# Routed expert layer: every expert on every token, or tiles of 256 rows of one expert each

## The reference

```python
x = x + ga * attention(h)                       # B, S, E = 4, 2048, 256
h = layernorm(x) * (1 + cb) + sb                # cb, sb, gb: one row of 256 per batch entry
probs = softmax(h @ gate_w.T + gate_b)          # over 8 experts
_, topi = top_k(probs, 2)
cw = einsum('bske,bsk->bse', one_hot(topi, 8), probs[..., :2])
out = 0
for e in range(8):
    t = relu(h @ w1[e] + b1[e]); t = relu(t @ w2[e] + b2[e]); t = t @ w3[e] + b3[e]
    out = out + cw[..., e:e+1] * t
x = x + gb * out
```

## Time and profile before

| | us |
|---|---|
| runs of the kernel before, median (lowest to highest) | 4469.58 (4466.67 to 4480.1) |
| the profiled execution, its own time | 4463.85 |
| its span, first to last instruction | 4462.3 |
| TensorE busy in the span | 3969.2 (89%) |
| VectorE, ScalarE, GpSimd busy | 2795.3, 1907.5, 1132.6 |
| granted clock of TensorE, mean | 0.965 |

### The profile page before, as it was taken

How to read it: one execution, slowest core, us unless ns; L and a number is a source line. 1 busy time by engine, 2 the same in 40 slices (tenths; PEclk the granted TensorE clock), 3 DMA queues, 4 the chain that set the end, 5 groups by cost and what they waited for, 6 DMA issues and landing times. The chain is left out here.

```text
span 4462.3 us, 182622 instructions
## 1 busy us (share of the span) xinstructions
PE 3969.2 (89%) x79696; PEld 3129.7 (70%) x79696; DVE 2795.3 (63%) x4823; ACT 1907.5 (43%) x2398; POOL 1132.6 (25%) x922
## 2 busy tenths in 40 slices
PE   6947999999999999999999999986699999999998
PEld 4537887778888778888778888775366566566565
DVE  5845666644667753566763666660678677687774
ACT  1301334453333454233444234444455555556555
POOL 1024222122221113221112322100133343333333
PEclk8968999998999999999999999998799999999999
DMA  4761110003110003110003100002411112112100
GB/s 131 207 158 48 31 30 25 17 27 96 33 32 22 22 21 103 34 33 22 21 22 96 40 23 28 17 6 48 98 25 43 30 25 48 25 30 43 24 10 10
DMA packets 212117, 201.07 MB, mean 45 GB/s; under 512 B 92048, under 2 KB 156156, under 8 KB 211324
## 3 DMA queue, kind: packets, MB, share of 16 engines
q1 hardware_dynamic: 195068, 154.30, 13.3%
q0 software_dynamic: 16256, 35.02, 2.6%
HBM read 128.69 MB, written 59.29 MB: 42 GB/s over the span
## 5 line engine op out<-in xcount | busy, mean ns | idle before, releaser
L739 ACT ACTIVATE att_pt<-att_ps 128x1024 f32<-128x1024 f32 x560 | 573.9, 1025 | 1246.0 <-PE att_ps L763 1245.9
L706 DVE TENSOR_TENSOR att_acc<-att_pm,att_acc 128x512 f32<-128x512 f32 x864 | 570.2, 687 | 361.9 <-PE att_pm L760 356.9
L714 DVE TENSOR_TENSOR att_acc<-att_pm,att_acc 128x512 f32<-128x512 f32 x1056 | 665.9, 684 | 171.2 <-PE att_pm L770 164.7
L760 PE MATMUL att_ps<-att_qx,table_x 68*128 68x64 f16 x8960 | 721.1, 194 | 0.0
L763 PE MATMUL att_ps<-att_qz,table_z 128*128 128x64 f16 x8960 | 718.3, 193 | 0.0
L742 ACT ACTIVATE att_pt<-att_ps 128x1024 f32<-128x1024 f32 x528 | 515.1, 1023 | 372.3 <-PE att_ps L770 371.5
L763 PEld LDWEIGHTS att_ps<-att_qz,table_z 128*128 128x128 f16 x8960 | 614.5, 99 | 0.0
L760 PEld LDWEIGHTS att_ps<-att_qx,table_x 68*128 68x128 f16 x8960 | 611.8, 98 | 0.1
L826 PE MATMUL att_po<-att_pt,att_vn 128*32 128x128 f32 x17408 | 593.6, 277 | 0.2 <-ACT att_pt L739 0.2
L664 POOL DMA_DIRECT2D s_m<-att_mrow x64 | 34.3, 535 | 1850.9 <-DVE att_mrow L722 1823.5
L756 PE MATMUL att_ps<-att_qs,att_kn 113*128 113x64 f16 x8960 | 451.6, 193 | 42.8 <-DMA att_qs<-s_m 32.6
(11 more groups left out here) (173 smaller groups left out, 5377.3 us busy)
## 6 DMA issues: line engine op xcount, KB each, us to landing
att_qe<-s_q SPq DMA_DIRECT2D x256, 128.0 KB
s_v<-prj_vx SPq DMA_DIRECT2D x32, 512.0 KB, 3.8
att_vn<-s_v SPq DMA_DIRECT2D x64, 256.0 KB, 3.4
s_o<-att_on POOLq DMA_DIRECT2D x64, 256.0 KB, 3.5
ffn_heads<-s_o SPq DMA_DIRECT2D x64, 256.0 KB, 5.0
att_qs<-s_q SPq DMA_DIRECT2D x128, 66.0 KB
prj_x<-in_x POOLq DMA_DIRECT2D x16, 512.0 KB, 4.6
att_kn<-s_k SPq DMA_DIRECT2D x128, 64.0 KB, 2.4
```

The costliest lines, as they stand in the source:

```text
L706: dve.tensor_tensor(held, got, held, ALU.max).then_inc(mx_done, 1)
L714: dve.tensor_tensor(held, got, held, ALU.max).then_inc(mx_done, 1)
L739: act.activation(pt[:, k % 2, :, t * 64:t * 64 + 64].rearrange("p h (x c) -> p x h c", x=2), ps[t][:, :, :].rearrange("p x (h c) -> p x h ...
L760: last = pe.matmul(groups[:, :, g], keep["table_x"][:, y:y + P], qx[0:G * D + G, s, x * (XQ // G) + g], start=False, stop=(g == XQ // G - ...
```

## The change

The last phase is replaced by `phase_moe`, written out without a loop, in three stages.

First, 16 chunks of 512 tokens are prepared as before (the sums are now inverted once for all chunks, with a pass through DRAM) and routed: `count` finds with matmuls against a triangle and a matrix of ones how many earlier tokens chose the same expert, which gives each token a row in the region of each of its two experts (`s_h` in DRAM). GpSimd scatters the normalised rows there, eight indirect transfers of 128 rows of 1 KB a chunk. `x1` goes to DRAM.

Second, a table of tiles is made from the counts: 71 tiles of 256 rows, each of one expert (2 x 8192 / 256 = 64, and up to seven more as each region is rounded up). The expert and the first row of a tile are read into registers with `value_load`, and the weights are addressed through them. TensorE transposes the tile's rows itself (`turn`). Results go to `s_y`.

Third, GpSimd gathers for each token its two rows of `s_y`, eight indirect transfers a chunk; ScalarE and VectorE weigh and add them, multiply by the gate and add `x1`.

In modulation the rows of `sb` and `1 + cb` are also made for all partitions, by 16 further matmuls. The diff, cut to its core:

```diff
-def phase_ffn(nc, io, keep):
+def phase_moe(nc, io, keep):
+    JT, TL = CH // P, 2 * P
+    NC, NBLK, ROWS = B * CPB, B * NB, B * S
+    NT = 2 * ROWS // TL + NX - 1
+    REGION = ROWS + TL
...
+            def _(sp):
+                def load_heads(c):
+                    if c >= 2:
+                        sp.wait_ge(wo_full, 2 * c - 2)
+                    sp.dma_start(heads[:, c % 2], io["s_o"][c * JT:(c + 1) * JT].rearrange("j c r t -> r (j c) t")).then_inc(heads_in[c % 2], 16)
+                    if c >= 1:
+                        sp.wait_ge(nrm_done, 2 * c)
...
+                    for q in range(4):
+                        sp.dma_start(inv[32 * q:32 * q + D], io["s_r"][c * JT:(c + 1) * JT, :, q].rearrange("j c t -> (j c) t")
...
+                for c in range(NC):
+                    if c + 1 < NC:
+                        load_x(c + 1)
+                        load_heads(c + 1)
+                    if c < NX:
+                        load_weights(c)
+                    sp.wait_ge(x1_done, c + 1)
+                    sp.dma_start(x1v[c], x1[:, c % 2]).then_inc(x1_out[c % 2], 16)
...
+                for e in range(NX):
+                    end = sp.value_load(tab_z[0:1, e:e + 1], min_val=0, max_val=NX * REGION)
+                    sp.dma_start(io["s_h"][bass.ds(end, TL)].rearrange("(j p) e -> p j e", p=P), zero[:, :, :]).then_inc(zero_out, 16)
...
+                def load_tile(t):
+                    start = sp.value_load(tab_r[0:1, t:t + 1], min_val=0, max_val=DUMMY + (NX - 2) * TL)
+                    if t >= 3:
+                        sp.wait_ge(xT_full, t - 2)
+                    sp.dma_start(xs[:, t % 3], io["s_h"][bass.ds(start, TL)].rearrange("(j p) e -> p j e", p=P)).then_inc(xs_in[t % 3], 16)
+
+                def store_tile(t):
+                    sp.wait_ge(y_done, t + 1)
+                    sp.dma_start(io["s_y"][t * TL:(t + 1) * TL].rearrange("(j p) e -> p j e", p=P), y[:, t % 2]).then_inc(y_out[t % 2], 16)
+
+                for t in range(3):
+                    load_tile(t)
+                for t in range(NT):
+                    if t + 3 < NT:
+                        load_tile(t + 3)
+                    store_tile(t)
...
+            def _(pool):
+                def scatter(c):
+                    pool.wait_ge(row_done, c + 1)
+                    for j in range(JT):
+                        for k in range(2):
+                            pool.indirect_dma_start(io["s_h"][:, :], bass.IndirectOffsetOnAxis(ap=row[:, c * JT + j, k:k + 1], axis=0),
+                                                    h[:, c % 2, j, :], None).then_inc(h_out[c % 2], 16)
...
+                for t in range(NT):
+                    pool.wait_ge(h1_hi, t + 1)
+                    if t >= 2:
+                        pool.wait_ge(p2_full, t - 1)
+                    pool.tensor_tensor(h1_s[:, t % 2, 1], h1_f[:, t % 2], h1_s[:, t % 2, 0], ALU.subtract).then_inc(h1_done, 1)
+                pool.wait_ge(back_done, 1)
+                for s in range(2):
+                    pool.wait_ge(y_out[s], (NT + 1 - s) // 2 * 16)
+                for c in range(NC):
+                    if c >= 2:
+                        pool.wait_ge(both_added, c - 1)
+                    for j in range(JT):
+                        for k in range(2):
+                            pool.indirect_dma_start(got[:, c % 2, j, k, :], None, io["s_y"][:, :],
+                                                    bass.IndirectOffsetOnAxis(ap=back[:, c * JT + j, k:k + 1], axis=0)).then_inc(got_in[c % 2], 16)
...
+            def _(dve):
+                for c in range(NC + 1):
+                    if c + 1 < NC:
+                        normalise(c + 1)
+                    if c < NC:
+                        residual(c)
+                    if c:
+                        route(c - 1)
+                    if c < NC:
+                        root(c)
+                    if c:
+                        choose(c - 1)
+                    if c < NC:
+                        scale(c)
+                    if c:
+                        assign(c - 1)
+                    if c < NX:
+                        split_weights(c)
...
+                for t in range(NT + AHEAD):
...
+                    k = t - 1
...
+                    k = t - 2
+                    if 0 <= k < NT:
+                        dve.wait_ge(p3_full, k + 1)
+                        if k >= 2:
+                            dve.wait_ge(y_out[k % 2], k // 2 * 16)
+                        dve.tensor_tensor(y[:, k % 2], halves(bank[6 + k % 2]), b3[:, bass.ds(expert.pop(k), 1), :].broadcast_to([P, 2, E]),
+                                          ALU.add).then_inc(y_done, 1)
...
+            def _(pe):
+                project(0)
+                for c in range(NC + 1):
+                    if c + 1 < NC:
+                        project(c + 1)
+                    if c:
+                        count(c - 1)
+                    if c < NC:
+                        logits(c)
...
+                def turn(t):
+                    pe.wait_ge(xs_in[t % 3], (t // 3 + 1) * 16)
+                    if t >= 2:
+                        pe.wait_ge(xT_done, t - 1)
...
+                turn(0)
+                for t in range(NT + 2):
+                    if t + 1 < NT:
+                        turn(t + 1)
+                    if t < NT:
+                        expert[t] = pe.value_load(tab_e[0:1, t:t + 1], min_val=0, max_val=NX - 1)
+                        pe.wait_ge(xT_done, t + 1)
+                        if t >= 2:
+                            pe.wait_ge(h1_f_done, t - 1)
+                        layer(t, 0, xT_s[:, t % 2], bank[2 + t % 2], p1_full)
+                    k = t - 1
+                    if 0 <= k < NT:
+                        pe.wait_ge(h1_done, k + 1)
...
+                        layer(k, 1, h1_s[:, k % 2], bank[4 + k % 2], p2_full)
+                    k = t - 2
+                    if 0 <= k < NT:
+                        pe.wait_ge(h2_done, k + 1)
...
```

More of the change, by code:

```diff
@@ new lines, in phase_moe @@
+        taken = a.sb("taken", [P, NX])
+        rowf = a.sb("rowf", [P, NBLK, 2])
+        probs = a.sb("probs", [P, NBLK, NX])
+        row, back = a.sb("row", [P, NBLK, 2], U32), a.sb("back", [P, NBLK, 2], U32)
+        part, total = a.sb("part", [P, NBLK, 2]), a.sb("total", [P, NBLK, 2])
+        regions = a.sb("regions", [P, NX])
+        steps = a.sb("steps", [P, NX, TMAX])
+        tiles, starts, moved, more = a.sb("tiles", [P, NX]), a.sb("starts", [P, NX + 1]), a.sb("moved", [P, NX]), a.sb("more", [P, NX])
@@ L960, in _, with load_weights @@
+                def load_weights(e):
                     if e >= 2:
@@ new lines, in _ @@
+                dve.memset(starts[:, 0:1], 0.0)
+                then(dve.reduce_sum(tiles[:, :], steps[:, :, :], AX.X))
+                for e in range(NX):
+                    then(dve.tensor_tensor(starts[:, e + 1:e + 2], starts[:, e:e + 1], tiles[:, e:e + 1], ALU.add))
+                first = starts[0:1, :].unsqueeze(1).broadcast_to([1, NT, NX + 1])
+                then(dve.tensor_tensor(begun[:, :, :], number[:, :, :], first, ALU.is_ge))
+                then(dve.reduce_sum(which[:, :], begun[:, :, :], AX.X))
@@ L1207, in _ @@
+                for c in range(NC):
+                    s = c % 2
+                    act.wait_ge(got_in[s], (c // 2 + 1) * 2 * JT * 16)
+                    for j in range(JT):
+                        last = act.activation(got[:, s, j, 0, :], got[:, s, j, 0, :], ACT.Copy, scale=probs[:, c * JT + j, 0:1])
+                    last.then_inc(first_done, 1)
             @block.tensor
@@ L1282, in _, with project @@
-                order(pe, piece, step, lambda e: None, piece_first=False)
+                pe.wait_ge(made, 3)
+                def project(c):
+                    if c >= 2:
+                        pe.wait_ge(att_done, 2 * c - 2)
+                    for m in range(2):
+                        pe.wait_ge(nrm_done, 2 * c + m + 1)
+                        for j in (2 * m, 2 * m + 1):
+                            for g in range(4):
+                                last = pe.matmul(halves(px[c % 2][m])[:, j % 2, :], heads[:, c % 2, 4 * j + g, :], wo[:, g, :], start=(g == 0), stop=(g == 3))
+                        last.then_inc(wo_full, 1)
@@ new lines, in count @@
+                def count(c):
+                    pe.wait_ge(both_done, c + 1)
+                    full, o = thirds(c % 2), both[:, c % 2]
+                    for j in range(JT):
+                        out = full[:, (JT + j) * NX:(JT + j + 1) * NX]
+                        for i in range(j):
+                            pe.matmul(out, ones[:, :], o[:, i, :], start=(i == 0), stop=False, skip_group_check=True)
+                        pe.matmul(out, before[:, :], o[:, j, :], start=(j == 0), stop=True, skip_group_check=True)
+                    for j in range(JT):
```

(9 more changed lines are left out.)

696 lines of the change are left out of this document (359 added, 337 removed).

## The result

The changed kernel takes 4535.5 us (median of 4 runs, 4524.47 to 4547.69) where the kernel before takes 4469.35 (4 runs): 1.0144 times, 95% interval 1.0113 to 1.0175. It is slower by 66 us, 1.4%. I had forecast 4620, 150 us more than before, so the direction and the range hold, and the change in time that I forecast is more than twice what came. The profiled execution of the changed kernel is its fastest, 4524.47.

A forecast was written before the change was run, and what follows sets the result against it. The prediction took TensorE to bound the replaced stage, some 1373 us. In its place 437 us of routing, 908 of tiles and 179 of gathers end at 4613, forecast 4620; own range 4520 to 4720, 8 in 10: 4410 to 4810.

The forecast's parts named there:

- 67 pitches: Expert stage: 67 tile loads that gate, one each 13.0 us, 871 us in all.
- what is late in the tile loop: Expert stage: each tile's load waits in SyncE's queue behind y and its store, so one whole load shows per tile.
- rival (b): Expert stage: loads come ahead of need and VectorE's chain sets the loop, 6.4 us a tile, 4178 us; chance 0.07.
- The gap: Expert stage: from third layer to next turn, through y, store, register load and load of rows, 5.7 us a tile.
- The burst: Expert stage: turn, TensorE's register load and three layers, 7.3 us a tile; 4.75 warm, 9.0 at half clock.
- my own formula: Expert stage: turn and layers with 5.5 us at half clock take 5.5 + (9.0 - 5.5) / 2 = 7.3 us.
- rival (a): Expert stage cold only in part or not at all, same 67 loads exposed: pitch 10.4, 4446 us; chance 0.14.
- (d): Expert stage: half clock throughout the tiles, pitch 14.7, +114 us, 4734 us; chance 0.12.
- The routing pitch: Routing stage: 21.5 us a chunk, bound by transfers, 16.7 and then 5 for normalise and residual; VectorE close behind.
- GpSimd's loop: Routing stage: scale, shift, eight scatters at 1.3 us, landing 3, scale again; 18.3 us a chunk, hidden.
- Between the stages: Routing to expert stage: last chunk to its rows 27 us, last scatter 13.5, zero blocks 14.5, first tile's preparation 7.
- Rival (c): Scatters and gathers: indirect transfers cost 2.3 us each, gathers +128, routing +72, last scatter +8, 4828 us; chance 0.14.

The follow-up runs named there:

- early load: Changed kernel with SyncE's load of tile t+4, before that of t+3, issued ahead of the store of tile t, same three buffers: 4190.3 us.
- third buffer alone: Changed kernel with three buffers instead of two for the normalised rows h in the routing stage: 4522.7 us.
- split alone: Changed kernel with VectorE forming the low halves of expert c-1's weights just before its wait for the counting of chunk c-1: 4517.0 us.
- combined kernel: Changed kernel with earlier load, new VectorE tile order, third h buffer, weight split before the counting wait, fp16 counting matrices and rearranged zero-block stores: 4021.1 us.

## Why the prediction was right and wrong

Its marks against those of the changed kernel, on the profile's clock:

| Mark | forecast | measured |
|---|---|---|
| first x1 stored | 3141 | 3142.0 |
| last x1 stored | 3463 | 3478.2 |
| last scatter landed | 3503.5 | 3523.0 |
| zero blocks there | 3518 | 3539.2 |
| third layer of tile 0 done | 3542 | 3560.7 |
| 67 pitches | 871 (13.0) | 762 (11.37) |
| first gather | 4434 | 4339.1 |
| 16 chunks of gathers | 166 | 171 |
| end | 4613 | 4523.0 |

**Right: what is late in the tile loop.** The load shows in full, 67 times. The early load took it away, and the tile fell to 6.30, which rival (b) had as 6.4. Rival (b) itself was rightly held unlikely, as the written order decides: it needs another order of the queue.

**Wrong in size: the tile's two terms.** This is the step that failed. The pitch was 13.0, and is 11.37; 67 x 1.63 = 109 us, more than the whole miss. (1) The gap: 5.7 forecast, 4.75 measured. The load was taken from the weights' transfers of 3.3 us plus 0.2 behind the store, and took 2.84 in the cycle shown, with nothing beside it but the store; the register load was 0.7 and is 0.57. (2) The burst: 7.3 forecast, 6.63 measured. Its part at full clock was 4.75 and is 5.00, by the run with TensorE kept busy. The time at half clock is what was too long: I gave it 5.5 us in every tile, and it is 4.1 on average, 5.7 to 6.1 in one tile of three and 2.7 to 3.4 in the others. By my own formula 4.1 gives 4.1 + (9.0 - 4.1) / 2 = 6.55. The run with TensorE kept busy prices half clock at 1.6 a tile, where the forecast had 2.55. I took the 5.5 from the start-up and from one 4.34 us gap. The rows were a pause after long full work and a start from nothing; the new state, a short gap every 11 us, had no row, and I took one of its ends as the value and the other for rival (a).

**Rivals (a) and (d).** (a), always warm, 10.4 and 4446, came out as the kernel with TensorE kept busy: 9.78 and 4429. (d), half clock throughout, didn't come: the window over the tiles has 0.80. The pitch measured lies between (a) and the forecast. That the time lies within my range of 4520 to 4720 is partly luck: I had given the tiles +-1 us, and 11.37 is outside that. The pitch alone would have put the time at 4620 - 109 = 4511; some 19 us that the other stages took longer brought it back in.

**The routing pitch: nearly right, for another reason.** 21.5 forecast, 22.4 measured; +15 us at the last x1. I had the transfers as the bound. In the changed kernel VectorE waited for inv 0.9 us in 260 us, so they weren't: VectorE's queue was, with waits that I had at 2 (the counting, up to 5.1) and at nothing (ScalarE's copy of the weights, 3.2 before each split). The transfers' 21.7 was close as a number, and they became the bound, at 20.8, when VectorE's queue was shortened. GpSimd's loop had 4.3 from the start of the last scatter to its landing, which took 6.3 to 8.9; it was as late as VectorE's queue. The third buffer alone gave no time that is clear of the runs' spread, and the split alone gave 10.5 us in the routing, until the buffer was late.

**Between the stages.** Last chunk to the end of its scatters: 40.5 forecast, 44.8 measured; zero blocks 14.5 and 16.2; fill 24 and 21.5. Small terms, right.

**Rival (c), dear indirect transfers.** It didn't come. A scatter takes 0.97 us in the median and 1.10 in the mean, a gather 0.96 and 1.02, and 0.30 of issue come to each; I had taken 1.3 for both together. Beside VectorE's normalise of 2.35 us single scatters take 1.65 and 1.97, which is the mechanism of (c) with 0.13 us on average where it had 1.0. The 3.1 us, for a transfer beside a vector operation, that the prediction quoted from the Trainium skill, "SBUF — State Buffer", section SBUF: two separate sides, was not seen here; the longest scatter took 1.97.

## What to carry to other kernels

When each piece of work carries its own load, look at which wait the load's issue stands behind in its queue, not at how many buffers there are: one step of order was worth 345 us with three buffers. Price an exposed wait twice, for itself and for what TensorE's clock loses by it, and take the clock's part from a gap of the same length and rhythm, or give it both ends. Where two loops of a stage are equally late, an edit that removes one moves its wait to the other and shows little or no time; the table of waits tells it, and the next edit collects. Count such a table with the waits that it puts down to issue, or the same wait looks as if it had grown.

## What the runs showed of the hardware that I had not expected

**Short operations of VectorE held by a pass of GpSimd.** From the changed kernel's timeline:

```profile
3308.45 2.69 DVE L1121 TENSOR_SCALAR moe_ve<-moe_mv 128x4 f32<-128x4 f32 x1
...
3308.74 2.36 POOL L1046 TENSOR_TENSOR moe_x<-moe_x,moe_gbo 128x1024 f32<-128x1024 f32 x1
```

An operation of 128x4 elements takes 2.69 us; it ends when GpSimd's pass does (3311.10), and in the combined kernel, where that pass comes later, it took 0.34 in the chunk at 3342. There a product of 128x32 took 1.49 on average, and 2.79 in the chunk where it ended with that pass; with the pass gone it takes 0.19 on average. The Trainium skill, "SBUF — State Buffer", section SBUF: two separate sides, describes it: VectorE, in a mode of two ports or with two inputs in SBUF, and GpSimd share a port pair that one of them holds for its whole instruction. The product of 128x32 has two such inputs, and the runs agree. The operation of 128x4 has one, and whether it ran in such a mode no trace shows; it was held all the same. The runs show the direction that costs more here: not the scatters, held by 1 us now and then, but VectorE's 0.2 us steps behind GpSimd's 2.36.

**The clock with short gaps.** In the tiles of the changed kernel TensorE idled 4.75 us, worked 6.63 and idled again, on average, and every burst had a stretch at half clock, 2.7 to 6.1 us of it, from before the turn (1.12 against 0.60) or from just behind it; with the same wait filled by unused matmuls, so that 0.85 of idle remained, the granted clock stayed at 1.00 over 652 us.

**Prices.** A register load on SyncE's queue 0.57 us, near the 600 ns that the prediction quoted from the Trainium skill, "DMA: Bandwidth & Descriptors", section Latency and other measured facts; an indirect transfer of 128 rows of 1 KB 1.28 from start to start; from the start of a chunk's last scatter to its landing 6.3 to 8.9 us in the routing with the loads beside it, and 3.6 where no load ran beside it (the last one, 3519.4 to 3523.0).
